# Grouped attention on one core: the score, row, value and projection work of a sequence dealt out over 64 beats, the output projection held inside group 1

## What is computed

```
sh1, sc1, g1, sh2, sc2, g2 = split(silu(c) @ wc.T + bc)
h = layernorm(x) * (1 + sc1) + sh1
q = (h @ wq.T) as (n, 4 groups, 4 heads, 32);  k, v = (h @ wk.T), (h @ wv.T) as (n, 4 groups, 32)
a = softmax(q . k / sqrt(32));  o = a . v
x = x + g1 * (o @ wo.T)
h = layernorm(x) * (1 + sc2) + sh2
x = x + g2 * (gelu(h @ w1.T + b1) @ w2.T + b2)
```

## Time and profile before

| | us |
|---|---|
| median of 3 runs | 1637.91 |
| the profiled execution | 1639.16 |
| its span, first to last instruction | 1637.4 |
| prologue and attention's lead-in | 94.5 |
| sequence 0, from its first score to that of sequence 1 | 86.6 |
| sequence 1 | 101.7 |
| sequences 2 to 6 | 98.9, 97.4, 97.4, 99.0, 98.9 |
| sequence 7, to its last score | 87.0 |
| from there to the MLP's first matmul | 25.3 |
| MLP | 750.7 |

### The profile page before, as it was taken

One profiled execution on the slowest core, in us unless ns is written; L12 is line 12 of the kernel. 1 busy time (PEld: TensorE's weight loads), 2 busy tenths in 40 slices (PEclk: granted clock), 3 DMA queues, 4 the chain that ended last, 5 costly groups with the idle time before them and its releaser, 6 DMA issues. The chain is left out here.

```text
span 1637.4 us, 21353 instructions
## 1 busy us (share of the span) xinstructions
PE 1519.6 (93%) x7013; PEld 1046.8 (64%) x7013; DVE 811.8 (50%) x1356; ACT 621.2 (38%) x1116; POOL 573.6 (35%) x222
## 2 busy tenths in 40 slices
PE   7789899898999989999877999999999999999996
PEld 4545464554655545455535888888888788888885
DVE  5377756666676666666654434242423324142412
ACT  5246555555556555555552231112111121112110
POOL 0036556566567557565561002020200202020202
PEclk9879999999999999999998999999999999999998
DMA  6221414023140412304023222020010102020100
GB/s 247 64 61 40 117 36 128 20 84 97 38 123 20 144 37 63 110 29 140 20 98 97 79 83 84 1 74 10 26 58 26 58 0 83 0 83 0 35 24 26
DMA packets 68280, 104.78 MB, mean 64 GB/s; under 512 B 10465, under 2 KB 19697, under 8 KB 68233
## 3 DMA queue, kind: packets, MB, share of 16 engines
q1 hardware_dynamic: 66192, 103.74, 20.8%
q10 hardware_dynamic: 2048, 0.53, 0.2%
HBM read 55.44 MB, written 16.81 MB: 44 GB/s over the span
## 5 line engine op out<-in xcount | busy, mean ns | idle before, releaser
L826 DVE TENSOR_REDUCE neg_max<-row_bank 128x1 f32<-128x512 f32 x512 | 345.6, 688 | 209.8 <-PE row_bank L1028 206.7
L1413 PE MATMUL acc<-w_t,hidden 128*128 128x512 f32 x1536 | 370.6, 390 | 7.7 <-DVE hidden L1330 7.7
L1403 PE MATMUL up<-h,w_t 128*128 128x512 f32 x1536 | 370.9, 391 | 0.0
L1413 PEld LDWEIGHTS acc<-w_t,hidden 128*128 128x128 f32 x1536 | 287.2, 188 | 69.8 <-DVE hidden L1330 10.7
L1403 PEld LDWEIGHTS up<-h,w_t 128*128 128x128 f32 x1536 | 287.4, 188 | 58.7
L705 ACT ACTIVATE probs<-key_bank 128x512 f32<-128x512 f32 x512 | 279.9, 594 | 109.7 <-PE key_bank L1041 101.3
L1328 DVE CAST hidden<-gelu_full 128x512 fp32r<-128x512 f32 x128 | 67.5, 527 | 443.2 <-ACT gelu_full L1274 441.6
L589 POOL TENSOR_TENSOR probs_sum<-probs_sum,probs 128x2048 f32<-128x2048 f32 x62 | 283.6, 4574 | 6.1 <-ACT probs L705 2.8
L1274 ACT ACTIVATE gelu_full<-up,bias_cols 128x512 f32<-128x512 f32 x128 | 88.3, 690 | 515.1 <-PE up L1403 515.1
L1028 PE MATMUL row_bank<-k_stack,q_stack 96*128 96x512 f32 x512 | 235.9, 463 | 23.4 <-DVE neg_max L826 15.4
L1041 PE MATMUL key_bank<-q_stack,k_stack 98*128 98x512 f32 x512 | 188.8, 439 | 44.6 <-ACT probs L705 24.0
(11 more groups left out here) (117 smaller groups left out, 1025.6 us busy)
## 6 DMA issues: line engine op xcount, KB each, us to landing
q_stack<-spare SPq DMA_DIRECT2D x384, 64.0 KB, 2.0
xa<-in_x_dram SPq DMA_DIRECT2D x8, 1024.0 KB, 9.8
resid<-in_x_dram SPq DMA_DIRECT2D x8, 1024.0 KB, 6.8
x_scratch<-resid SPq DMA_DIRECT2D x8, 1024.0 KB, 4.3
xa<-x_scratch SPq DMA_DIRECT2D x8, 1024.0 KB, 5.6
spare<-in_L_cond_w_dram SPq DMA_DIRECT2D x32, 256.0 KB, 3.0
resid<-x_scratch SPq DMA_DIRECT2D x8, 1024.0 KB, 6.8
out_dram<-y SPq DMA_DIRECT2D x8, 1024.0 KB, 4.2
```

The source lines that it names most:

```text
L826: nc.vector.tensor_reduce(out=neg_max[:, g % 2, i:i + 1], in_=row_bank[(g + i) % 2][:, :], op=ALU.max, axis=AX.X, negate=True).then_inc(ro ...
L1403: last = nc.tensor.matmul(up[j % 2][:, :], w1_t[i][:, kt, j * P:j * P + P], h[k][:, kt, :], start=(kt == 0 and n == 0), stop=(kt == KD - 1 ...
L1413: last = nc.tensor.matmul(acc[tt][:, :], hidden[j % 2][i][:, tt * P:tt * P + P], w2_t[k][:, j, :], start=(j == 0 and n == 0), stop=(j == N ...
```

## The change

The order of slots gives way to an order of **beats**, 64 in a sequence (16 in a group, beat n = 4 kt + r of its group). A beat is one score, one row, the values of the tile before where r = 1, the parts that a new `FILL` gives the beat, and sums at beat 8. A part is a quarter of a unit (three matmuls, letters a to d), or a whole transpose.

- `row_items` gives each beat one row, and beat 6 two. Beats 11 to 15 take the first 5 rows of the group after the next (`AHEAD` becomes 5), and beat 10 takes `turn_max` in place of a row.
- ACT and DVE take a unit 1 or 2 beats after its last part (a transpose is modulated after 1 beat, copied after 2, split after 3).
- The steps from sums to the result are spread: logarithm at beat 8, exponential at 9, refine at 10, the reciprocal (its own function now) and divide at 11, `attn_high` and `attn_low` at 15; of group 0 at beats 34 and 35 of the sequence, after O3.
- T0 to T3 move to group 0, at beats 6, 10, 11 and 15. O0 starts at beat 16 and O3's last quarter ends in beat 32. K, Q0, V, Q1, Q2 run from beat 34 to 54.
- The normalisation moves a sequence earlier: statistics in beats 39, 42, 43, 44, moments and `add_eps` in 47, shift in 52, the norm steps one by one in beats 54, 55, 59, 63. Those of sequence 1 are made in the lead-in, the four `bn_stats` and `moments` on DVE ahead of the row maxima of group 0 but one.
- POOL does the three additions of a group together and the residual additions after them: 0 after group 0, 1 after group 1, 2 and 3 after group 2; `rstd_of` before these.
- SP loads the input right after T3, and stores and loads the residual only after `stack_q(1)`.

```diff
+FILL = {
+    (0, 0): ("VT", "", "Q3a", ""),
+    (0, 1): ("Q3b", "Q3c", "Q3d T0", ""),
+    (0, 2): ("", "", "T1", "T2"),
+    (0, 3): ("", "", "", "T3"),
+    (1, 0): ("O0a", "O0b", "O0c", ""),
+    (1, 1): ("O0d O1a", "O1b", "O1c", ""),
+    (1, 2): ("", "", "", "O1d"),
+    (1, 3): ("O2abcd", "", "", "O3abc"),
+    (2, 0): ("O3d", "", "Kabcd", "Q0abc"),
+    (2, 1): ("", "Q0d", "Va", ""),
+    (2, 2): ("", "", "Vbcd Q1a", "Q1b"),
+    (2, 3): ("", "Q1c", "Q1d", "Q2a"),
+    (3, 0): ("", "Q2b", "", "Q2c"),
+    (3, 1): ("", "", "Q2d", ""),
+    (3, 2): ("", "", "", ""),
+    (3, 3): ("", "", "", ""),
+}
...
+                def beat(b, n, u, has_last, has_next):
...
+                    scores(b, g, kt, r, has_last)
+                    for row in rows_in(b, n, has_next):
+                        if row[2] < ROWS:
+                            rows(*row)
+                    if r == PV_BEAT and kt > 0:
...
                         values(b, g, kt - 1, is_first=not has_last and g == 0)
...
+                    for name, tiles in fill(n, has_last, has_next):
+                        do(name, tiles, b, u)
+                    if (kt, r) == SUM_AT and prev:
                         sums(*prev, is_first=not has_last and g == 1)
+                    for row in rows_in(b, n, has_next):
+                        if row[2] == ROWS:
+                            turn_max(*row[:2])
...
                     stack_q(u, 3)
-                    if has_last:
-                        store_x1(b - 1)
                     if has_next:
-
-                        sp.wait_ge(proj_taken["dve"], u.taken("K"))
-                        stack_k(0)
-                        stack_k(1)
-                        stack_q(u, 0)
-                        stack_q(u, 1)
-                    if has_last:
-                        sp.wait_ge(x1_stored, b * 16)
-                    load_resid(b)
-                    if has_next:
+                        sp.wait_ge(proj_ready, u.ready("T3"))
                         if is_second_last:
                             load_x(x1_dram, 0)
                         else:
                             load_x(x, b + 2)
-                        sp.wait_ge(keys_scored, exps_no(b, HKV - 1, 0))
+                        sp.wait_ge(proj_taken["dve"], u.taken("K"))
+                        stack_k(0)
+                        stack_q(u, 0)
+                        sp.wait_ge(keys_scored, exps_no(b, 2, 0))
+                        stack_k(1)
+                        stack_q(u, 1)
+                    if has_last:
+                        store_x1(b - 1)
+                        sp.wait_ge(x1_stored, b * 16)
+                    load_resid(b)
+                    if has_next:
+                        sp.wait_ge(keys_scored, exps_no(b, 3, 0))
                         stack_k(2)
                         stack_q(u, 2)
```

More of the change, by code:

```diff
@@ new lines @@
+GROUP = TT * R
+PV_BEAT = 1
+PV_COPY = 2
+SUM_AT = (2, 0)
+LN_AT = (2, 0)
+INVERT_AT = (2, 1)
+REFINE_AT = (2, 2)
+RECIP_AT = (2, 3)
+DIVIDE_AT = (2, 3)
+HIGH_AT = (3, 3)
+LOW_AT = (3, 3)
+FIRST_HIGH = 34
+FIRST_LOW = 35
+TURN_BEAT = 10
+TWO_ROWS = 6
+ACT_LAG, DVE_LAG, COPY_LAG, TURN_LAG = 1, 2, 2, 3
+STATS_AT = (39, 42, 43, 44)
+MOMENTS_AT = 47
+EPS_AT = 47
+SHIFT_AT = 52
+NORM_AT = (54, 55, 59, 63)
+COND_AT = 2
+RESID_AFTER = {0: (0,), 1: (1,), 2: (2, 3)}
+TAKER = {"T": "dve", "V": "act", "K": "dve", "Q": "dve", "O": "dve"}
@@ new lines, in parts_of, with fill @@
+def parts_of(token):
+    if token == "VT" or token[0] == "T":
+        return token, range(1)
+    name = token.rstrip("abcd")
+    return name, ["abcd".index(c) for c in token[len(name):]]
+def fill(n, has_last, has_next):
+    if n < 0 or n >= BEATS:
+        return []
+    slot, r = divmod(n, R)
+    found = [parts_of(token) for token in FILL[divmod(slot, TT)][r].split()]
+    return [(name, quarters) for name, quarters in found
+            if (has_last or name[0] != "O") and (has_next or name not in ("K", "Q0", "Q1", "Q2", "V"))]
@@ L51, with ended @@
+def ended(n, has_last, has_next):
+    return [name for name, quarters in fill(n, has_last, has_next)
+            if name == "VT" or name[0] == "T" or KD - 1 in quarters]
 class Units:
@@ L81, in seq_order @@
 def seq_order(has_last, has_next):
-    return [n for g in range(HKV) for kt in range(TT) for n in fill(g, kt, has_last, has_next)]
+    return [name for n in range(BEATS) for name in ended(n, has_last, has_next)]
 def before_units():
@@ L102, with row_items @@
 ROWS = R * TT
+def row_items():
+    items, at = [[] for _ in range(GROUP)], TURN_BEAT + 1
+    for i in range(ROWS + 1):
+        beat = at % GROUP
+        items[beat].append((2 if at < GROUP else 1, i))
+        if not (beat == TWO_ROWS and len(items[beat]) == 1):
+            at += 1
+    return items
+ROW_ITEMS = row_items()
+AHEAD = sum(1 for beat in ROW_ITEMS for ahead, _ in beat if ahead == 2)
 def row_no(b, g, i):
@@ L878, in before @@
                     u = before_units()
[L879 removed]
+                    for kt in range(KD):
+                        h_low(0, kt, u)
                     k_low(0, u)
@@ L883, in before @@
                     q_low(0, 2, u)
-                    for i in range(ROWS):
+                    for tt in range(TT):
+                        tile_stats(1, tt)
+                    dve.wait_ge(stats_done, 2 * TT)
+                    row_max(0, 0, 0)
+                    moments(1)
+                    for i in range(1, ROWS):
                         row_max(0, 0, i)
```

326 lines of the change are left out of this document (145 added, 181 removed).

## The result

The changed kernel takes 1570.28 us (median of 4 runs, 1570.09 to 1571.06), the kernel before beside it 1638.7 (4 runs, 1637.48 to 1644.13). The ratio is 0.9577, interval 0.9555 to 0.9599. The forecast was 1579 with a range of 1552 to 1625.

The account below looks back on a forecast made before the run. PE was taken to bound the kernel, with about 15 us of each 97.4 us inner sequence waiting. Inner sequences −47, sequence 0 −6, sequence 7 −10, lead-in +3.5, and −1.25 to the median, gave 1579 us from 1639.2; range 1552 to 1625.

Parts of the forecast that it names:

- The inner sequence: Sequences 1 to 6: 91 us each, ends 87 and 96; six together from 593.3 to 546, −47 us.
- The named stalls: Row waiting 1.38 us behind bn_stats on DVE, score waiting 1.62 behind norm steps on ACT; both were to go.
- The sum over fours: Largest of PE, DVE and ACT work over each four beats, added over an inner sequence: 86.8 us.
- the middle between pairs and fours: Inner sequence taken as 91 us, between the largest-engine sums over two beats (94.7) and four beats (86.8).
- the sum over pairs: Largest engine's work over each two beats, added over an inner sequence: 94.7 us; as a rival 1618 us, chance 0.13.
- rival 4: Beats flow so well that the granted clock never falls: inner sequence 87 us or less, 1550 us in all; chance 0.06.
- What bounds the ends of groups 0 and 3: Beats 8 to 15: DVE late, with 10.4 us against PE's 7.9 in group 0, 8.3 against 6.9 in group 3.
- Sequence 0: First sequence: 86.6 us before, by fours 74.0, by pairs 82.9; taken as 80.5, −6 us.
- rival 2: Maxima's DMAs meet the residual's at sequence boundaries: 3.5 us for each of 7, +24, 1603 us; chance 0.10.
- Rival 3: Beats run in lockstep, each costing its slowest engine: inner sequence 103.1 us, 1669 us in all, slower; chance 0.09.
- The waits costed at nothing: O3's gate (0 to 1.2 us), shift_of at beat 52 (at most 1), POOL's sums, SP's queue, the maxima: taken as hidden.
- Sequence 7: Last sequence: 87.0 us to 77, −10, with POOL bounding beats 40 to 56; 5.4 of it one wait for maxima.

Follow-up runs that it names:

- e1: Kernel before, slots kept, with only the statistics put one to a row and the norm steps dealt over two slots: 1619.43 us, ratio 0.9853.
- e2: Changed kernel with the four bn_stats together in beat 44 and the four norm steps together in beat 63: 1592.0 us, ratio 0.9695.
- e5: Changed kernel with the maxima's DMAs issued by SP, ahead of the residual's store and load, instead of by ACT: 1554.59 us, ratio 0.9468.
- e9: e4 with the edit of e5 (maxima's DMAs issued by SP): 1621.53 us, ratio 0.9908.
- e7: e3 with the edit of e5 (maxima's DMAs issued by SP): 1597.32 us, ratio 0.9749.
- e10: e5 with six quarters of projections moved into or towards the beats where PE still waits: 1564.76 us, ratio 0.9548.
- e12: e5 with two of the result's four DVE steps on 32 of 512 columns, leaving out the refinement for the others: 1546.29 us, ratio 0.9438.
- e3: Changed kernel with each projection made whole in one beat instead of in quarters: 1648.68 us, ratio 1.0054.
- e4: Changed kernel with PE's order alone altered to two scores, then two rows, then the units of both beats: 1678.71 us, ratio 1.0253.
- e6: Kernel before with one SP wait, so the last sequence's MLP weight loads follow the first score of group 3: 1633.72 us, ratio 0.9978.

## Why the prediction was right, and where its steps were off

**The inner sequence** was forecast at 91 and is 87.9 without a fall of the clock and 89.5 with one. Three things stand behind the 59.4 us of the six:
- *The named stalls* are gone as said. At equal clock that is worth 0.9 us of a sequence in the old order (e1) and 2.4 in the new one (e2), 5 to 14 us for six; the 21 us by which both runs move hold falls of the clock too.
- *The sum over fours* was nearly the truth: 86.8 by the sum, 87.9 measured, 87.2 in e5. The fours that the sum gave to PE came out at 4.4, 5.8, 5.3, 6.1, 4.9, 8.0, 8.7, 7.6, 5.2 and 4.5 us, for 4.0, 5.7, 5.1, 6.0, 4.5, 7.9, 8.5, 7.2, 5.1 and 4.5. Where it gave them to DVE or ACT, work slid into the next four: group 0's last two took 4.9 and 5.4 for 5.7 and 4.7, group 3's last two 4.4 and 4.2 for 5.0 and 3.4. The mis-sized term was the middle between pairs and fours. Two banks of each kind let PE make up a long beat within about four, if score and row alternate; e9 shows that the sum over pairs (94.7) is reached when PE itself goes in pairs (95.7). It is no rule for every fill: e7 took 93.4 for a sum over fours of 88.2, and e10 88.7 for 84.9. That it fits the change so well is in part luck.
- *The clock* had ten falls in these sequences before, one of them twice as long, and has four now: 10.5 us of the 59. I had left it out of the sum and made it a rival of its own (rival 4); it came half.

One part of the gain had no term. The sum was made for the order after, so the forecast doesn't hang on it, but the account of what PE waits for before does. In the kernel before, first scores of a group waited for their maxima, and I had a row only for the one of 5.4 us in sequence 7. The timeline of sequence 4 of the kernel before has three more, and the list of waits the total:

```profile
479.08 0.73 PE L1041 MATMUL key_bank<-q_stack,k_stack 98*128 98x512 f32 x2 [0.50 <-DMA q_stack<-max_row]
...
500.14 0.72 PE L1041 MATMUL key_bank<-q_stack,k_stack 98*128 98x512 f32 x2 [0.26 <-DMA q_stack<-max_row]
...
553.89 0.79 PE L1041 MATMUL key_bank<-q_stack,k_stack 98*128 98x512 f32 x2 [0.99 <-DMA q_stack<-max_row]
...
PE key_bank L1041 <- DMA q_stack<-max_row: 19.8, 24, 5.4
```

With `turn_max` at beat 10 these 1.75 us of a sequence are gone; in the changed kernel one wait is left, that of sequence 0.

**What bounds the ends of groups 0 and 3.** The prediction named DVE, "in beats 8 to 15 of groups 0 and 3". For beats 12 to 15 of group 3 that holds: e5 leaves them as they are (4.17 and 4.16 us), and with less for DVE they take 3.68 (e12). For beats 12 to 15 of group 0 it was ACT. The step that failed there is the count of ACT: 0.6 us for each copy and nothing for the issue of the two DMAs, 1.18 us by the row I had quoted myself. e5 took that time away, 5.40 to 4.34 us, and DVE was next (4.08 in e12). The issue of DMAs was counted for SP (0.6 us each) and forgotten for ACT.

**Sequence 0**: forecast 80.5, measured 84.4, of which 3.5 is rival 2 in the one place where no store holds the residual's load back. Without it, and without ACT's issue (e5), it is 78.4.

**Rival 2** was given 0.10 at "3.5 us for each of 7 boundaries". It came at one boundary, and at the other six it was missed by 1.1 us of issue. e3 and e4 show it come at all seven (26.5 and 22.4 us on PE's own list) by nothing but a shift of beats. The mechanism and the price were right; what I didn't see is that it decides by the order of issue, so that an unrelated edit can trigger it.

**Rival 3**, the lockstep, is refuted for the change as it is (89 against 103.1). e4 and e3, in which the alternation or the quarters are given up, are slower than the slots, but only together with the meeting of DMAs and the clock: without these, e9 and e7 are still faster than the kernel before (0.9908 and 0.9749).

**The waits costed at nothing.** `gate` of O3 waited 0.32 us for POOL (said: 0 to 1.2), and the row maximum behind it wasn't late for PE. SP's queue and the stacking of Q0 held nobody, and POOL's sums nobody in the inner sequences. The lead-in is 3.0 longer, forecast 3.5; its row, beside 3.71 in the kernel before:

```profile
81.80 11.12 PE L1098 MATMUL row_bank<-k_stack,q_stack 96*128 96x512 f32 x14 [6.23 <-DVE neg_max L901]
```

**Sequence 7** is 75.7, forecast 77. POOL bounds beats 40 to 56 as said: the sums of beats 40 and 56 start 15.2 us apart (at 770.46 and 785.65, forecast 15.3), and PE waits for the second:

```profile
785.65 1.06 PE L1130 MATMUL sum_bank<-probs_sum,ones 128*32 128x512 f32 x8 [0.59 <-POOL probs_sum L650]
```

The DMAs of the last maxima are issued at 774.7, the weights' loads from 793.6 on, and no score of the sequence waits for a DMA. By e6 3.7 of the 5.4 us were the loads' doing, and 1.7 the late turn, which the earlier `turn_max` took as well. Another 4.5 of the 11.3 us gained are the clock's, which the forecast didn't have.

**The rule weighed.** The last four beats of group 1 hold 29 matmuls of scores, rows and projections, beside those of the values, and nothing but PE bounds them. By 0.233 us they were forecast at 7.9 and took 7.97; nine of them in a row, from 492.98 to the score at 495.07, are 0.232 apart. By the 216 ns of the Trainium skill ("TensorE: Matmul & The Clock Gate", "Back-to-back issue gap"), which that section calls the gap of a single matmul, the four beats would be 7.4 (an estimate), and the 131 ns that it has for a stream with weight loads is further off still: here the trace disagrees with the page.

## What to carry to other kernels

Where each unit of one engine is taken by another through two banks, order the work so that kinds alternate singly and cut long units into quarters between them; then the time can come near the largest engine's sum over about four steps (87.9 for 86.8 here), and not before (pairs cost 67 us, whole units 43). Take that sum as the least, not as the time: e10 and e7 stayed 4 and 5 us above theirs. Compare orders by sequences at the same granted clock, or a few falls pass for a gain. Count a DMA issued from a computing engine as 0.6 us of that engine, and let an idle queue issue it. Before a small DMA on which the next step hangs, look at what large transfer is issued near it: if only a microsecond of luck keeps it ahead, put the order into a queue, as e5 does.

## What the runs showed of the hardware that was not expected

- Two 8 KB DMAs land in 1.8 to 1.9 us when issued 1.1 us ahead of a 1 MB load, in 3.5 to 7.5 when issued 0.2 us behind the first of the loads (e3, at the ends of sequences 1 to 5), in 6.9 to 8.3 when issued 0.3 us behind the 1 MB one (e4), and still in 5.4 to 6.7 when 2.9 us behind it (sequence 0 of the changed kernel). They are on ACT's queue and the load is on SP's. A 1 MB store issued 3.3 us ahead of them (531.24 in the changed kernel) does them no harm; such stores land after 4.2 us on the median, the residual's loads after 7.8.
- In three places of the changed kernel the granted clock falls to 1.2 GHz for about 3.4 us though PE has had no longer idle than 0.49 and 0.91 us within 3.5 (the window ahead of the fall has PE busy for 2.51 us). In e5, where both waits are gone, the profiled execution has no fall in an inner sequence. Waits as such don't tell: e9 has none either, with this wait in sequence 4:

```profile
485.77 0.50 PE L1125 MATMUL key_bank<-q_stack,k_stack 98*128 98x512 f32 x1 [1.26 <-ACT probs L783]
```
